# Weighted sum of gathered tokens: weights stationary and 512 columns moving, with a transpose behind it, in a one-core Trainium2 kernel

## The reference, cut to what matters

```python
# x: (4, 512, 24, 24). First a state-space block over 2305 steps per batch, added to x (not touched here).
t = _to_tokens(x)                      # (4, 576, 512)
t = t + _L0_ffn_ref(_ln_t(t), memory_tokens, memory_router)

def _L0_ffn_ref(x, memory_tokens, memory_router):      # memory_tokens: (256, 128, 512)
    ...
    x0 = x[:, 0, :]
    router_scores = x0 @ memory_router
    top_vals, top_idx = jax.lax.top_k(router_scores, 8)
    router_weights = jax.nn.softmax(top_vals, axis=1)
    gathered = memory_tokens[top_idx]                  # (4, 8, 128, 512)
    combined = jnp.einsum('bk,bktd->btd', router_weights, gathered)
    return x.at[:, 1:T + 1, :].set(combined)           # T = 128
```

## Time and profile before

| | |
|---|---|
| time, median of three runs | 1304.27 us (1303.02 to 1305.35) |
| the profiled execution | 1302.34 us |
| its span in the trace | 1300.6 us |
| TensorE, matmuls busy | 1100.8 us (85%) |
| VectorE busy | 1157.0 us (89%) |
| GpSimd busy | 1110.7 us (85%) |
| ScalarE busy | 806.6 us (62%) |

### The profile page before, as it was taken

One profiled execution on the slowest core, in us unless ns is written; L12 is line 12 of the kernel. 1 busy time (PEld: TensorE's weight loads), 2 busy tenths in 40 slices (PEclk: granted clock), 3 DMA queues, 4 the chain that ended last, 5 costly groups with the idle time before them and its releaser, 6 DMA issues.

```text
span 1300.6 us, 13356 instructions
## 1 busy us (share of the span) xinstructions
PE 1100.8 (85%) x3818; PEld 660.8 (51%) x3818; DVE 1157.0 (89%) x1345; ACT 806.6 (62%) x1496; POOL 1110.7 (85%) x747
## 2 busy tenths in 40 slices
PE   6588888888888988988988988988988888887997
PEld 4344554544544544544544544545545545444887
DVE  1399999999999999999999999999999999999751
ACT  2476765766766666766666666666757657656230
POOL 4299899898898898898898898898998998988750
PEclk8789999999999898898998998999998998998998
DMA  6221321222221221221222212213212213215351
GB/s 160 75 96 53 104 97 58 87 94 77 80 98 68 92 99 57 99 99 61 98 82 78 99 64 96 99 57 104 99 56 104 99 56 116 96 63 168 115 159 30
DMA packets 64539, 116.80 MB, mean 90 GB/s; under 512 B 34218, under 2 KB 47954, under 8 KB 64466
## 3 DMA queue, kind: packets, MB, share of 16 engines
q1 hardware_dynamic: 64466, 115.96, 26.3%
HBM read 108.47 MB, written 7.47 MB: 89 GB/s over the span
## 4 chain that ended last, share of the span: by engine, by line
POOL 29%; PE 22%; DVE 21%; issue 21%; ACT 6%; POOLq 0%; SPq 0%; DVEq 0%; DMA 0%; ACTq 0%
POOL SCAN L413 16%; DVE SCAN L967 13%; PE Yp L693 8%; POOL SCAN L425 6%; DVE SCAN L922 4%; PE PP L772 3%; PE PP L839 3%; PE PP L722 2%; PE PP L819 2%; POOL XN L450 1%; PE PP L812 1%; POOL GATES L418 1%; DVE GATES L951 1%; ACT SGZ L598 1%; POOL XN L441 1%
## 5 line engine op out<-in xcount | busy, mean ns | idle before, releaser
L967 DVE TENSOR_TENSOR_SCAN SCAN<-DA,CAR,SCAN 128x384 f32<-128x384 f32 x768 | 729.8, 1000 | 38.4 <-POOL SCAN L425 36.5
L413 POOL TENSOR_TENSOR SCAN<-SCAN,CS 128x768 f32<-128x768 f32 x384 | 693.9, 1821 | 27.2 <-DVE SCAN L967 26.8
L490 ACT ACTIVATE DA<-UDT,A 128x384 f32<-128x384 f32 x768 | 441.8, 581 | 389.6 <-DVE SCAN L967 386.3
L693 PE MATMUL Yp<-SCAN,IDENT 128*128 128x384 f32 x1536 | 593.7, 512 | 97.5 <-POOL SCAN L413 89.6
L693 PEld LDWEIGHTS Yp<-SCAN,IDENT 128*128 128x128 f32 x1536 | 289.7, 198 | 304.9 <-POOL SCAN L413 143.5
L922 DVE TENSOR_TENSOR SCAN<-UDT,BB 128x768 f32<-128x768 f32 x288 | 268.7, 933 | 11.1 <-PE BB L675 9.2
L425 POOL TENSOR_TENSOR SCAN<-UDT,BS 128x768 f32<-128x768 f32 x96 | 175.4, 1827 | 0.0
L839 PE MATMUL PP<-XN,WT 128*128 128x384 f32 x384 | 139.8, 499 | 0.0
L839 PEld LDWEIGHTS PP<-XN,WT 128*128 128x128 f32 x384 | 75.8, 199 | 56.6 <-issue 11.8
L445 POOL TENSOR_TENSOR UDT<-UDT 128x768 f32<-128x768 f32 x24 | 43.5, 1811 | 69.9 <-DVE UDT L1056 69.9
L675 PE MATMUL BB<-PT,SEL 96*128 96x384 bf16 x288 | 98.3, 342 | 4.6 <-DVE SCAN L922 4.6
(11 more groups left out here) (161 smaller groups left out, 1155.4 us busy)
## 6 DMA issues: line engine op xcount, KB each, us to landing
CS<-bc_rows SPq DMA_DIRECT2D x96, 768.0 KB, 4.0
BS<-bc_rows SPq DMA_DIRECT2D x24, 768.0 KB, 6.0
out<-XN SPq DMA_DIRECT2D x32, 192.0 KB, 2.4
X<-in_x SPq DMA_DIRECT2D x24, 192.0 KB, 3.6
X<-in_L_ffn_memory_tokens SPq DMA_DIRECT2D x16, 256.0 KB, 3.0
XN<-in_L_ffn_memory_tokens SPq DMA_DIRECT2D x16, 256.0 KB, 3.1
bc_rows<-XDT SPq DMA_DIRECT2D x24, 48.0 KB, 1.5
X<-in_L_ffn_memory_router SPq DMA_DIRECT2D x1, 512.0 KB, 3.8
```

The source lines that it names most:

```text
L413: pool.tensor_tensor(M[:, n1 % MRING], HB[:, n1 % HRING], over_halves(CS[:, n1 % CRING]), ALU.mult).then_inc(m_ready, 1)
L490: act.activation(DA[:, h, 0:T], DT[:, par, h], ACT.Exp, scale=A[:, h, n:n + 1])\
L693: last = pe.matmul(Yp[:, h, 0:T], IDENT[:, :], M[:, n3 % MRING, h], start=n3 == 0, stop=n3 == NS - 1)
L967: dve.tensor_tensor_scan(HB[:, s % HRING, h], DA[:, h, 0:T], HB[:, s % HRING, h], CAR[:, ds(J * NS * HALVES + s * HALVES + h, 1)], ALU.mul ...
```

## The change

The sum is turned round. The diagonal weight matrices become the stationary operand, and a whole gathered block, 128x512 in one row of contiguous channels, moves: eight matmuls of 512 columns for a batch in the place of 32 of 128 columns. The result then has tokens on partitions. ScalarE copies it to an SBUF tile `MIXT` (in the tile `DT`, channel order kept), and four transposes per batch, each with every fourth channel of `MIXT` stationary and the identity moving, put it back into the same PSUM bank with channels on partitions, where `add_routed` reads it as before. The weight matrices are made by ScalarE, eight instructions of 128 columns for a batch, and no longer by one instruction of VectorE. The tables give the steps: `WEIGH` (ScalarE), `MIX` (TensorE), `MIXED` (ScalarE's copy), `TURN` (TensorE) and `ADD` (VectorE). On SyncE the third load of output rows of the last unit moves from ahead of the third gather to behind it.

```diff
@@ -124,6 +124,7 @@
+        MIXT = DT[:, 0].rearrange("p h t -> p (h t)")[:, 0:DIM].rearrange("p (c q) -> p q c", q=Q)
@@ -178,18 +179,18 @@
-        COMBINE = {(COMB, 1 + q): [(0, q)] for q in range(Q)}
-        COMBINE.update({(COMB, 6 + q): [(1, q)] for q in range(Q)})
-        COMBINE.update({(COMB, 12 + q): [(2, q)] for q in range(Q)})
-        COMBINE.update({(COMB + 1, 3): [(3, 0), (3, 1)], (COMB + 1, 5): [(3, 2), (3, 3)]})
-        ADD = {(COMB, 5): 0, (COMB, 10): 1, (COMB + 1, 1): 2, (COMB + 1, 13): 3}
+        WEIGH = {(COMB, 0): 0, (COMB, 2): 1, (COMB, 7): 2, (COMB, 14): 3}
+        MIX = {(COMB, 1): 0, (COMB, 4): 1, (COMB, 12): 2, (COMB + 1, 0): 3}
+        MIXED = {(COMB, 2): 0, (COMB, 5): 1, (COMB, 13): 2, (COMB + 1, 1): 3}
+        TURN = {(COMB, 3): 0, (COMB, 6): 1, (COMB, 14): 2, (COMB + 1, 2): 3}
+        ADD = {(COMB, 4): 0, (COMB, 7): 1, (COMB, 15): 2, (COMB + 1, 3): 3}
@@ -350,9 +351,9 @@
             load_c(UNITS - 1, 1, 2)
-            load_c(UNITS - 1, 1, 3)
             sp.wait_ge(g_used, 1)
             gather(2)
+            load_c(UNITS - 1, 1, 3)
             sp.wait_ge(g_used, 2)
             gather(3)
@@ -615,6 +616,23 @@
+                if (J, s) in WEIGH:
+                    b = WEIGH[(J, s)]
+                    act.wait_ge(f_dve, 9)
+                    if b == 3:
+                        act.wait_ge(g_used, 1)
+                    for kk in range(TOPK):
+                        last = act.activation(WI[:, b % 3, kk], IDENT[:, :], ACT.Copy,
+                                              scale=WBC[:, b * TOPK + kk:b * TOPK + kk + 1])
+                    last.then_inc(w_spread, 1)
+                if (J, s) in MIXED:
+                    b = MIXED[(J, s)]
+                    act.wait_ge(g_used, b + 1)
+                    if b:
+                        act.wait_ge(mix_turned, b)
+                    act.activation(MIXT, comb_bank(b).rearrange("p (c q) -> p q c", q=Q), ACT.Copy).then_inc(mix_copied, 1)
@@ -759,21 +777,26 @@
-                for b, q in COMBINE.get((J, s), ()) if isinstance(J, int) else ():
-                    if q == 0:
-                        pe.wait_ge(f_dve, (10, 11, 12, 13)[b])
-                        if b == 1:
-                            pe.wait_ge(comb_done, 1)
-                        if b == 2:
-                            pe.wait_ge(z_clamped, UNITS)
-                        pe.wait_ge(g_loaded[b], 16 * TOPK)
+                if (J, s) in MIX:
+                    b = MIX[(J, s)]
+                    pe.wait_ge(w_spread, b + 1)
+                    if b:
+                        pe.wait_ge(comb_done, b)
+                    if b == 2:
+                        pe.wait_ge(z_clamped, UNITS)
+                    pe.wait_ge(g_loaded[b], 16 * TOPK)
                     for kk in range(TOPK):
-                        last = pe.matmul(comb_bank(b)[:, q * P:(q + 1) * P],
-                                         G[b % 2][:, kk].rearrange("p (c q) -> p q c", q=Q)[:, q],
-                                         WI[:, b % 3, kk], start=kk == 0, stop=kk == TOPK - 1)
-                    if q == Q - 1:
-                        last.then_inc(g_used, 1)
+                        last = pe.matmul(comb_bank(b), WI[:, b % 3, kk], G[b % 2][:, kk],
+                                         start=kk == 0, stop=kk == TOPK - 1)
+                    last.then_inc(g_used, 1)
+                if (J, s) in TURN:
+                    b = TURN[(J, s)]
+                    pe.wait_ge(mix_copied, b + 1)
+                    for q in range(Q):
+                        last = pe.transpose(comb_bank(b)[:, q * P:(q + 1) * P], MIXT[:, q], IDENT[:, :])
+                    last.then_inc(mix_turned, 1)
@@ -897,16 +920,10 @@
-            def weigh(b):
-                dve.tensor_tensor(WI[:, b % 3], IDENT[:, :].unsqueeze(1).broadcast_to([P, TOPK, P]),
-                                  WBC[:, b * TOPK:(b + 1) * TOPK].unsqueeze(2).broadcast_to([P, TOPK, P]),
-                                  ALU.mult).then_inc(f_dve, 1)
-
             def add_routed(b):
-                dve.wait_ge(g_used, b + 1)
+                dve.wait_ge(mix_turned, b + 1)
@@ -1032,13 +1049,8 @@
-                if at(J, COMB) and s < BATCH - 1:
-                    dve.wait_ge(f_dve, 9)
-                    weigh(s)
-                if isinstance(J, int) and (J, s) in ADD:
+                if (J, s) in ADD:
                     add_routed(ADD[(J, s)])
-                if at(J, COMB) and s == 6:
-                    weigh(3)
```

More of the change, by code:

```diff
@@ L180, in build @@
         idx_ready = sem("idx_ready"); g_loaded = [sem(f"g_loaded{b}") for b in range(BATCH)]
-        g_used = sem("g_used"); comb_done = sem("comb_done")
+        g_used = sem("g_used"); w_spread = sem("w_spread"); mix_copied = sem("mix_copied"); mix_turned = sem("mix_turned"); comb_done = sem("comb_done")
         N_WLOADS = 8
```

## The result

| | before | after |
|---|---|---|
| time, median (range) | 1304.79 us (1303.02 to 1305.35), four runs | 1285.79 us (1283.56 to 1287.25), four runs |
| ratio | | 0.9863, 95% interval 0.9852 to 0.9875 |
| span of the profiled execution | 1300.6 us | 1282.6 us |

The changed kernel is 19.0 us (1.4%) faster; 21.0 us under a median of 1304.27, or 1283, was forecast, and the time lies in the stated range. In a second measurement, with the experiments, the same kernel took 1287.53 us beside 1303.11, a ratio of 0.9889 (0.9872 to 0.9905), so the gain is 15 to 19 us.

What follows compares the result with a forecast made beforehand. From 1210 us TensorE's queue was taken to set the end; its 26.7 us saving became 21.8 at the end, 21.0 after 0.8 for the clock. 1304.27 - 21.0 = 1283.3, forecast 1283 us, range 1280 to 1287 (chance 0.69).

Steps and rivals of the forecast that it cites:

- MIX at 6.88 us: TensorE's new sum per batch: 16 passes of 512 columns at 0.43 us; upper bound 0.54 us a pass if loads were uncovered.
- TURN at 0.9 us: TensorE's four transposes per batch, 0.9 us together; bounds 0.11 to 0.226 us each.
- WEIGH at 2.33 us: ScalarE's eight 128-column instructions making a batch's weight matrices: 2.33 us, bounds 2.1 to 4.0.
- MIXED at 0.59: ScalarE's copy of a sum from PSUM: 0.59 us, bounds 0.5 to 1.2.
- The clock at 0.8 us: TensorE's clock dips at the gaps ahead of MIX(0) and MIX(2): 0.8 us for both together, at most 3.4 for one.
- Rival 2: The clock dips at both gaps, as long as the dip seen: 6.0 us more, 1289.3 us; chance 0.11.
- WEIGH(2) at 0.2 us: Between MIX(1) and MIX(2), ScalarE's WEIGH(2) makes the decay of step 9 late by 0.2 us.
- VectorE idle behind MIX(0): VectorE out of work from about 1204.5 to 1211 us, waiting for Yp queued behind MIX(0).
- the tie at MIX(3): Three engines arrive together ahead of MIX(3): TensorE at 1255.9 us, ScalarE's WEIGH(3) at 1255.85, VectorE's add(2) at 1255.6.
- the uncovered x2: Between MIX(3) and the mean, x2 takes 0.84 us on the path; half of batch 3's sum hid it before.
- SyncE's cover: Gathers of batches 2 and 3 land 13 us before MIX(2) and MIX(3); no cost unless over 10 us late.
- Rivals 1, 3, 4 and 5: 1: full saving, 1277.6 us, chance 0.08; 3: dear ScalarE, 1288.9, 0.08; 4: half clock, 1327, 0.02; 5: slow MIX, 1313, 0.02.

Runs made afterwards that it cites:

- b_contig: The kernel before with the sum's stationary quarter taken as 128 neighbouring channels instead of every fourth: 1280.15 us beside 1302.72, ratio 0.9824.
- b_step2: The kernel before with the sum's stationary quarter taken as every second channel of one half, 8 bytes apart instead of 16: 1280.91 us beside 1303.56.
- x_turnmm: The changed kernel with TURN as plain fp32 matmuls against the identity instead of transposes: 1286.49 us beside 1303.56.
- x_flat: The changed kernel with ScalarE's copy of the sum written as one contiguous row of 512: 1285.42 us beside 1303.11, ratio 0.9877.
- after_again: The changed kernel unaltered, measured again with the experiments: 1287.53 us beside 1303.11 for the kernel before.
- x_loadc: The changed kernel with the third load of output rows ahead of the third gather again: 1287.86 us beside 1303.56, ratio 0.9868.
- x_best2: The changed kernel with MIX(0) one step later, contiguous copy, gate copies before step 12's decay, and weight matrices made by VectorE: 1280.78 us beside 1303.56, ratio 0.9822.

## Why the prediction was right

The mechanism was right: TensorE's queue set the end, the 16-byte step made L772 dear, and most of TensorE's saving arrived. The table follows its own steps, which leave out its 0.8 us for the clock. The anchor before MIX(0) (the end of the second decay, 1200.12 in the prediction) lies at 1201.24, since this execution was 1.1 us later before it reached the touched code:

| step | predicted | measured |
|---|---|---|
| decay's end to MIX(0) | 2.3 us | 2.4 us |
| MIX(0) to MIX(1) | 14.8 | 16.4 |
| MIX(1) to MIX(2) | 24.7 | 25.1 |
| MIX(2) to MIX(3) | 14.0 | 14.2 |
| MIX(3) to the mean | 13.2 | 13.2 |
| mean to the end | 9.7 | 10.0 |
| together | 78.7 | 81.4 |

Two of the recorded partial sums are off by 0.1 us (the terms up to MIX(1) give 1217.3, those from MIX(3) to the mean 13.1), and the two slips cancel.

- **MIX at 6.88 us** was right, 6.94 measured; the taken lower bound (no uncovered load) was the true one.
- **Why L772 was dear**: the step of 16 bytes, argued from 0.226 us a pass beside 0.11, is now shown by b_contig, and its limits by b_step2 and x_turnmm.
- **TURN at 0.9 us** was wrong: 0.47, the lower end. I priced a transpose by a plain fp32 matmul with the same step, and x_turnmm shows that the two differ by nearly a factor of two a pass. The transposes of the program's start, 0.22 us each, were no support: that stretch ran at half pace, although the clock column has 1.00 for it. Eight passes of 96 columns took 2.03 us there and 1.03 in the last unit of the same kernel:

```profile
9.01 2.03 PE L819 MATMUL PP<-SQ,MEANW 128*128 128x96 f32 x8 [1.27 <-ACT SQ L624]
...
1255.31 1.03 PE L812 MATMUL PP<-SQ,MEANW 128*128 128x96 f32 x8
```

  Of the two rules of the Trainium skill weighed there, the one of TensorE: Matmul & The Clock Gate, section LDWEIGHTS (a load goes by its columns, 107 ns for 128, with no term for the step) fits the pace of the transposes, 0.12 us, though their load records last 210 ns. The one of SBUF — State Buffer, section Door 1 (a penalty at each new 16-byte line) fits the plain fp32 passes at 0.226 us. Neither holds for both.

  Four transposes at 0.9 instead of 0.47 us are 1.7 us too many. About half of such time reaches the end by x_turnmm, so I estimate 0.8 us there. That hid about as much of the clock's cost, and the total is so much nearer by luck.
- **WEIGH at 2.33 us** measured 2.43. **MIXED at 0.59** measured 1.09, near the upper bound of 1.2; the strided read for which no row stood doubled it. x_flat shows that it touched nothing; MIXED(2), named as the one place on the path, was not on it.
- **The clock at 0.8 us** was the term that was mis-sized. The stretch that I called the nearer, the one that cost nothing, was not: behind a gap of 2.9 us or more the stream lost 1.5 to 3.1 us in seven of seven cases. In the profiled execution MIX(0) lost 1.5 us and the variance at the end 0.2 more than in the kernel before, 1.7 where I had 0.8. The 0.9 us beyond are half of the 1.9 us by which this execution came later than forecast within the last unit. after_again lost at both gaps, and its 1287.53 us lie just above the 1280 to 1287 to which I gave 0.69. Rival 2, which had 6.8 us for the two gaps together, was right in kind, too high for this execution and nearer to what after_again lost (4.7 us).
- **WEIGH(2) at 0.2 us** between MIX(1) and MIX(2), where 0.4 us are missing. VectorE and ScalarE set this stretch, as forecast, but the chain goes through all eight instructions of WEIGH(2), 2.37 us. With the matrices made by VectorE (x_weighdve) the stretch takes 24.8 us instead of 25.1, so WEIGH(2) fits most of the miss; no run isolates it.
- **VectorE idle behind MIX(0)**, 7.7 us, came as forecast (1206 to 1214 where I had 1204.5 to 1211), and so did the tie at MIX(3), the uncovered x2 (0.91 us of waiting) and SyncE's cover (the gather of batch 2 starts at 1220.5 us, MIX(2) at 1245.2). That cover rests on the new order: x_loadc shows MIX(2) waiting for the gather in the old order.
- Rivals 1, 3, 4 and 5 did not come.

What stays open is how much of the 3.4 us between the two measurements of the changed kernel's gain the clock explains; only one execution of each was profiled.

## What to carry to other kernels

Look at the pace of a matmul stream against its columns before restructuring it: 0.226 us a pass for 128 columns said that the stationary operand's layout was being paid, and the cure here was a form that loads contiguous columns and leaves the step to a transpose. When a stream is made longer and denser, ask which engine's input is queued behind it: one position in the order was worth 3 us here, and one order on another engine 2.3. Close the gaps ahead of a dense stream (filling one with idle matmuls kept the clock there, and the time did not show it). When work is moved between engines, price it by what that engine does at that moment, since the same four instructions were free on VectorE in one order and cost some 3 us in the next.

## What the runs showed of the hardware that I had not expected

- A stationary fp32 operand of a plain matmul: 0.11 us a pass with contiguous columns, 2.04 us for 16 passes with a step of 8 bytes, 0.226 us a pass with 16 bytes. A transpose with the same 16-byte step took 0.12 us.
- ScalarE's copy of 512 fp32 elements from PSUM took 1.09 us walked in steps of 16 bytes on both sides and 0.59 us in a row.
- Ahead of the streams of MIX the granted clock fell in all seven gaps of 2.9 us and more, in three of six of 2.29 us and in none of nine with 1.78 us or less; a stream of 7.13 us then took up to 10.15 us. Elsewhere a gap of 2.69 us cost nothing (x_best2), and behind one of 1.20 us at the end of the program, after others of 0.58 and 0.91 us, the clock had fallen (L835, 1.98 us instead of 1.13).
